# Eight of the sixteen weight halves of a graph kernel are loaded and split during the node stage instead of the prologue

## The reference

```python
# layer 1: graph convolution with self loops
H = X @ W
out = segment_sum(H[src] * (dinv[src] * dinv[dst])[:, None], dst) + b
x = layernorm(x + leaky_relu(out, 0.01))
# layer 2: attention of each edge's target to the edge
r = concat([x[src], x[dst], edge_feat]) @ Wr.T + br
q, k, v = x @ Wq.T + bq, r @ Wk.T + bk, r @ Wv.T + bv
a = softmax_over_edges_of_dst((q[dst] * k).sum_per_head / 8)
out = segment_sum(v * a, dst) @ Wo.T + bo
x = layernorm(x + batchnorm(x + out))
```

## Time and profile before

| | us |
|---|---|
| median of 3 runs | 1370.69 |
| lowest and highest run | 1368.41, 1375.07 |
| the profiled execution | 1368.55 |
| its span, first to last instruction | 1366.8 |
| PE busy in the span | 1293.5 (95%) |
| DVE, POOL, ACT busy | 1079.3, 815.7, 631.2 |

### The profile page before, as it was taken

One profiled execution on the slowest core, in us unless ns is written; L12 is line 12 of the kernel. 1 busy time (PEld: TensorE's weight loads), 2 busy tenths in 40 slices (PEclk: granted clock), 3 DMA queues, 4 the chain that ended last, 5 costly groups with the idle time before them and its releaser, 6 DMA issues. The chain is left out here.

```text
span 1366.8 us, 21920 instructions
## 1 busy us (share of the span) xinstructions
PE 1293.5 (95%) x6534; PEld 1044.9 (76%) x6534; DVE 1079.3 (79%) x2018; ACT 631.2 (46%) x1187; POOL 815.7 (60%) x752
## 2 busy tenths in 40 slices
PE   7898989999999799999999999999999999869987
PEld 6787878888888688888888888888888888644333
DVE  6577638999998425788988888888888888968877
ACT  3477646777777412223332333222332233246877
POOL 3566426667676534556655666666666654567875
PEclk9999999999999799999999999999999999969999
DMA  8798875777776423434344444444444443839886
GB/s 265 261 342 304 269 238 186 241 246 239 247 243 226 168 79 85 133 98 146 117 132 128 133 129 138 139 133 131 137 139 139 139 139 93 289 120 371 276 282 229
DMA packets 128301, 257.96 MB, mean 189 GB/s; under 512 B 21459, under 2 KB 21907, under 8 KB 128114
## 3 DMA queue, kind: packets, MB, share of 16 engines
q1 hardware_dynamic: 97490, 175.31, 38.9%
q0 software_dynamic: 29920, 80.38, 20.2%
q10 hardware_dynamic: 832, 1.57, 0.4%
HBM read 197.18 MB, written 73.60 MB: 198 GB/s over the span
## 5 line engine op out<-in xcount | busy, mean ns | idle before, releaser
L207 PE MATMUL ps<-w_lo,w_hi 128*128 128x512 f32 (+2 forms) x1140 | 415.3, 364 | 6.4 <-DVE w_lo L1457 3.6
L208 PE MATMUL ps<-w_hi,w_lo 128*128 128x512 f32 (+2 forms) x1140 | 410.0, 360 | 0.0
L209 PE MATMUL ps<-w_hi 128*128 128x512 f32 (+2 forms) x1140 | 409.8, 359 | 0.0
L207 PEld LDWEIGHTS ps<-w_lo,w_hi 128*128 128x128 f32 x1140 | 216.7, 190 | 38.7 <-DVE w_lo L1457 4.9
L209 PEld LDWEIGHTS ps<-w_hi 128*128 128x128 f32 x1140 | 216.4, 190 | 32.1
L208 PEld LDWEIGHTS ps<-w_hi,w_lo 128*128 128x128 f32 x1140 | 217.0, 190 | 29.9
L1241 POOL TENSOR_TENSOR acc_x<-acc_x,node_rows 128x512 f32<-128x512 f32 x72 | 116.0, 1610 | 81.2 <-DMA node_rows<-x_table 77.0
L907 POOL TENSOR_TENSOR node_y<-node_z,node_x 128x512 f32<-128x512 f32 x79 | 102.8, 1301 | 72.1 <-issue 38.9
L207 PE MATMUL ps<-w_lo,agg_hi 128*128 128x512 f32 x316 | 132.0, 418 | 1.5 <-DVE agg_lo L971 1.5
L209 PE MATMUL ps<-w_hi,agg_hi 128*128 128x512 f32 x316 | 125.1, 396 | 0.0
L208 PE MATMUL ps<-w_hi,agg_lo 128*128 128x512 f32 x316 | 124.5, 394 | 0.0
(11 more groups left out here) (271 smaller groups left out, 2887.5 us busy)
## 6 DMA issues: line engine op xcount, KB each, us to landing
node_x<-in_x SPq DMA_DIRECT2D x79, 256.0 KB, 3.8
x_table<-node_x SPq DMA_DIRECT2D x79, 256.0 KB, 2.1
node_rows<-x_table SPq DMA_DIRECT2D x79, 256.0 KB, 8.3
coef_all<-coef_table SPq DMA_DIRECT2D x38, 512.0 KB, 7.1
edge_part<-part SPq DMA_DIRECT2D x40, 256.0 KB, 4.2
out_dram<-rows_over_w_lo SPq DMA_DIRECT2D x40, 256.0 KB, 6.2
node_x<-in_ea SPq DMA_DIRECT2D x38, 256.0 KB, 4.9
msg_table<-dst_rows_and_msg SPq DMA_DIRECT2D x38, 256.0 KB, 4.9
```

The costliest lines, as they stand in the source:

```text
L207: pe.matmul(to, left[0], right[1], start=first, stop=False, skip_group_check=onto)
L208: pe.matmul(to, left[1], right[0], start=False, stop=False, skip_group_check=onto)
L209: return pe.matmul(to, left[0], right[0], start=False, stop=last, skip_group_check=onto)
```

## The change

Halves 0 to 7 are handled as before (`EARLY = 8`). Halves 8 to 15 leave the prologue on SP, ACT and DVE. In the node stage SP loads them whole, one every eight steps (half 8 ahead of step 11, the others at steps 16, 24, ... 64). From step 16 to step 79 each step splits one piece of 128 columns: ACT copies it to `w_hi` between `agg_hi` and the root, and POOL subtracts it one step later, behind its gather. PE waits for the 64 pieces in front of the edge stage's first product. Semaphores are renumbered to match.

```diff
+EARLY = 8
+PIECE = 128
 # prologue, SP / ACT / DVE
-            if j + 6 < 2 * NW:
+            if j + 6 < EARLY:
                 load_weights(j + 6)
-            if j < LATER:
+            if j + 2 < EARLY:
                 weights_high(j + 2)
-            if j < LATER:
+            if j + 2 < EARLY:
                 weights_low(j + 2)
 # node stage
+        FIRST_PIECE = 16
+        AFTER_PIECES = FIRST_PIECE + (2 * NW - EARLY) * WH // PIECE
+        def has_piece(j):
+            return not isinstance(j, int) or FIRST_PIECE <= j < AFTER_PIECES
 # SP
+            if isinstance(j, int) and j == 11:
+                load_later(0)
+            if s == 0 and not (isinstance(j, int) and (j < FIRST_PIECE or j + 8 >= AFTER_PIECES)):
+                sp.wait_ge(later_in, (j - FIRST_PIECE) * 2 + 16)
+                load_later((j - FIRST_PIECE) // 8 + 1)
 # POOL, behind the gather
+            if has_piece(j - 1):
+                pool.wait_ge(g.w_hi_ok, j - FIRST_PIECE + EARLY)
+                nc.gpsimd.tensor_tensor(piece(g.w_lo, j - 1), piece(g.over_lo, j - 1), piece(g.w_hi, j - 1).bitcast(F32), ALU.subtract).then_inc(g.w_lo_ok, 1)
 # ACT, between agg_hi and the root
+            if has_piece(j):
+                if s == 0:
+                    act.wait_ge(later_in, (j - FIRST_PIECE) * 2 + 16)
+                nc.scalar.copy(piece(g.w_hi, j), piece(g.over_lo, j)).then_inc(g.w_hi_ok, 1)
 # PE, in front of the edge stage's first product
+                pe.wait_ge(g.w_lo_ok, EARLY + (2 * NW - EARLY) * WH // PIECE)
```

More of the change, by code:

```diff
@@ L49 @@
 WH = K * D // 2
-LATER = 2 * (NW - 1)
+EARLY = 8
+PIECE = 128
 HOMES = 12
@@ L314, in prologue_stage @@
         RUNS, ENDS, CARRIED, CARRY_TURNED, COUNTED, TURNED, DEGREES, ROOTS, DINV_DST = 2, 4, 5, 6, 7, 8, 9, 10, 11
-        w_in = g.w_in = [sem(f"weights_in{s}") for s in range(NW)]
-        w_hi_ok, w_lo_ok = sem("weights_high"), sem("weights_low")
+        w_in = g.w_in = [sem(f"weights_in{s}") for s in range(5)]
+        w_hi_ok, w_lo_ok = g.w_hi_ok, g.w_lo_ok = sem("weights_high"), sem("weights_low")
         def by_k(row):
@@ L433, in weights_high @@
             if i < 2:
-                act.wait_ge(w_in[(0, NW - 1)[i]], 16)
+                act.wait_ge(w_in[(0, 4)[i]], 16)
             else:
-                act.wait_ge(w_in[i // 2], 48 if i // 2 == NW - 1 else 32)
+                act.wait_ge(w_in[i // 2], 32)
             nc.scalar.copy(g.w_half(g.w_hi, i), g.w_half(g.over_lo, i)).then_inc(w_hi_ok, 1)
@@ L461, in scalar_program @@
         for i in range(2):
-            g.load_half(act, g.w_half(g.over_lo, i), i).then_inc(w_in[(0, NW - 1)[i]], 16)
+            g.load_half(act, g.w_half(g.over_lo, i), i).then_inc(w_in[(0, 4)[i]], 16)
             act.dma_start(ea_rows[:, i, :], g.ea[i * P:(i + 1) * P, :]).then_inc(ea_in[i], 16)
@@ L864, in node_stage, with piece @@
         ps_t, ps_o = ps[0:2], ps[4:8]
+        later_in = g.later_in = sem("later_weights_in")
+        FIRST_PIECE = 16
+        AFTER_PIECES = FIRST_PIECE + (2 * NW - EARLY) * WH // PIECE
+        def has_piece(j):
+            return not isinstance(j, int) or FIRST_PIECE <= j < AFTER_PIECES
+        def piece(half, j):
+            return half[:].rearrange("p w n -> p (w n)")[:, bass.ds((j - FIRST_PIECE) * PIECE + EARLY * WH, PIECE)]
         b_in = g.const_in
@@ L883, in sync_program, with load_later @@
     def sync_program(sp):
+        def load_later(i):
+            g.load_half(sp, g.w_half(g.over_lo, i + EARLY), i + EARLY).then_inc(later_in, 16)
         def step(j, s, on):
+            if isinstance(j, int) and j == 11:
[3 more added lines that the diff above has]
+                load_later((j - FIRST_PIECE) // 8 + 1)
             if on(0) and not (isinstance(j, int) and j < RX):
@@ L1868, in finish_stage @@
         SCALE_IN_PSUM, SCALE_ROW = 1, 2
-        y_out = g.w_in[2:6] + g.row_out + g.u_out
-        y_before = [32] * 4 + [16 * NB] * 4
+        y_out = g.w_in[1:5] + g.row_out + g.u_out
+        y_before = [32] * 3 + [16] + [16 * NB] * 4
         mine = g.step_v
```

## The result

The changed kernel takes 1363.42 us in the median of nine runs (1357.95 to 1367.62), the kernel before 1370.93 us beside it (1368.19 to 1375.07). The ratio is 0.994, 95% interval 0.9922 to 0.9959: a gain of 0.41 to 0.78%, or 5.6 to 10.7 us. The forecast was 1365.4, a gain of 5.3, which lies just under that interval. The profiled execution of the changed kernel is the slowest of its nine, 1367.62 us (span 1365.9), so the two profiles are compared stage by stage and not by their ends.

A forecast was written before the change was run, and what follows sets the result against it. PE was taken as the bound, with only its idle time to win: six prologue waits for DVE's scans give -5.3 us, the node stage costs 0, so 1370.69 - 5.3 = 1365.4 us, range 1359 to 1372.

The forecast's parts named there:

- The six waits: Prologue, 98 to 151 us: PE waits 5.3 us for DVE's scans, queued behind a subtraction waiting for ACT's rounding; all disappear.
- The wait changes hands: Prologue rival: the gathers or ACT's scaling take over PE's 5.3 us, so no change; half the gain left gives 1368; 13%.
- The term of 5.3 us: Prologue: removing the six PE waits gains 5.3 us, bounds 0 and 5.3 + 1.3, and arrives at the node stage.
- Traffic at nothing: Prologue: eight loads of 0.5 MB leave SP and the queue; no PE wait names a transfer, so counted at nothing.
- cost 0: Node stage: the added ACT copy, POOL subtraction and loads cost nothing; a step stays at 3.24 us.
- POOL's piece: Node stage: a subtraction of 128 columns on POOL, taken as 0.40 us, standing until node_agg ends.
- over 0.8: Node stage: node_agg longer than 0.8 us was named as a sign of a wrong prediction; 0.75 was expected.
- The sum: Node stage, POOL's step: piece runs 0.40 after node_agg ends, node_y begins some 0.5 behind; POOL needs 2.92 of 3.24 us.
- The slower rival: Node stage: POOL's piece holds DVE's node_agg (16 us, 1381) or sets the step (37 us, 1402); 10%.
- the 0.72: Node stage: POOL has room for a piece of 0.40 + 0.32 = 0.72 us; above that it sets the step.
- 0.58 a step: Node stage: a piece taking the full 1.30 makes POOL's step 3.82 us, adding 0.58 in each of 64 steps.
- the order mends itself: Node stage: node_y is tied to node_agg's end, so delaying one moves the other and the piece keeps arriving behind node_agg.

The follow-up runs named there:

- first: The changed kernel with the eight loads left in the prologue, only the splitting in the node stage: 1364.48 us, ratio 0.9968 to the kernel before.
- sixth: Loads in the prologue, twelve halves instead of eight split in the node stage, in 48 pieces of 256 columns: 1366.96 us, ratio 0.9986 to the kernel before.
- fourth experiment: Loads in the prologue, node-stage pieces of 512 columns in 16 steps instead of 128 in 64: 1381.08 us, ratio 1.0098 to the kernel before.
- third: The changed kernel with DVE instead of POOL subtracting each piece, directly behind node_agg: 1363.31 us, ratio 0.9964 to the kernel before.
- seventh: The changed kernel, with the six halves left in the prologue's loop subtracted one step later: 1361.44 us, ratio 0.9948 to the kernel before.
- fifth experiment: The changed kernel with POOL's piece between node_y and the gather instead of behind the gather: 1362.56 us, ratio 0.9953 to the kernel before.

## Why the prediction was right, and where its sizes were off

**The mechanism.** Right in the main. The six waits are gone, nothing took their place, the gain reached the node stage, and moving only the subtraction in DVE's order gives half of it. The prediction gave the waits this one cause; the loads are a second (below). That the time lies in the range says little, for the range of 1359 to 1372 holds no change too; the waits and the experiments carry the account. "The wait changes hands" is refuted: PE has no wait from 98 to 151 us.

**The term of 5.3 us.** Too small, and the step that failed is taking PE's recorded waits as the whole price of standing. Steps 8 to 15 got 6.58 us shorter for 5.35 recorded, 0.2 more at each of six waits. At the earlier trace rows the group of transposes in front began at 102.25,

```profile
102.25 0.60 PE L606 MATMUL ps<-ident,acc_x 128*128 128x128 f32 x4
```

and the next at 104.18, 1.93 later; undisturbed the pitch is 0.43, so the stall cost 1.50 and not 1.33. A last matmul's recorded 0.60 lies 0.17 over the pitch, and hides that much of the idle time behind it. (The Trainium skill, Perfetto Trace Analysis, section "Tensor Engine Instruction (MATMUL, LD_WEIGHTS)", says that the end of a matmul is computed and not observed. The rows agree: the recorded 0.60 outlasts the next start by 0.17.) The waits' price should have been read as pitch against pitch: 5.3 + 6 x 0.2 = 6.5.

**Traffic at nothing.** This was wrong. Steps 8 to 15, in the profiled execution of each kernel:

| loads of halves 8 to 15 | splitting of halves 8 to 15 | steps 8 to 15, us | PE idle in them |
|---|---|---|---|
| prologue | prologue (kernel before) | 52.9 | 5.35 |
| prologue | prologue, subtraction a step later | 49.6 | 2.49 |
| prologue | node stage (first, sixth and fourth experiment) | 47.3, 48.8, 49.5 | 0.70, 1.90, 2.75 |
| node stage | node stage (the change; third, seventh and fifth experiment) | 46.3, 46.3, 46.3, 46.5 | 0 |

With the splitting gone, the loads still cost 1.0 to 3.2 us. No wait of PE names a transfer; it stands one or two links behind PE, under ACT's or the scans' name: from 60 to 150 us ACT stands 4.7 to 11.3 us for the stores of the sums with the loads in the prologue, and 0 to 1.6 without. Whether the stores are late from the traffic or from their place behind the loads on SP, no run tells. The forecast did not suffer, by luck: the change takes the splitting and the loads away together, and the recorded waits held the price of both.

**The earlier start.** The loop began 2.08 us earlier, which no term had. It also began 1.1 to 2.1 us earlier in the seven other kernels, one of which is the kernel before itself up to the loop's start. So 1.4 of it (49.37 against 50.77) appeared without any of the change: the start differs that much from one execution to another.

**The node stage.** Right in what counts: cost 0, step 3.24, `node_agg` 0.75 in most steps. The first `node_agg` was to come at 190 and came at 186.58, by the two items above. ACT's copy took 0.31 us, not 0.25, and was hidden. POOL's piece takes 0.46 to 0.47 alone, not 0.40, and yet `node_y` starts 0.30 behind `node_agg` and not 0.5: some 0.15 of the piece lies beside `node_agg`'s end. The sum had counted all of it behind. In the changed kernel 7 of 79 `node_agg` took 0.85 to 1.05 us (the prediction had named over 0.8 as a sign of being wrong), 1.3 us too long in all, and PE has no recorded wait for them. The rule of the Trainium skill that was weighed there (SBUF — State Buffer, "Who interferes with whom") agrees with both orders seen: the piece 751 ns where it came second, `node_agg` 2.17 where the piece ran first. The page also infers that DVE's `tensor_tensor` takes only the read side of that interface and that generating descriptors needs the write side; carried over to `node_agg`, which has two SBUF inputs as well, a gather should not hold it, and the 0.75 beside a gather agrees.

**The slower rival.** Pieces of the size that it named do lose, but more than it was priced. Pieces of 256 (0.76 us alone, over the 0.72) lost 7.2 us in the profiled execution where the excess over POOL's room gives 48 x 0.04 = 2; POOL's round with a free piece of 256 takes 3.14 of 3.24, so the room was larger than worked out, and the loss is `node_agg` held. Pieces of 512 lost 16.9 us where the prediction's 0.58 a step gives 16 x 0.58 = 9.3. The working had let `node_y` overlap what it waits for: once the piece goes first, `node_agg`'s rest is one more link in the ring. Its statement that the order mends itself held in most steps with pieces of 128, and in none of the first 14 with pieces of 512.

**Open.** With a piece of 256 behind the gather, `node_agg` is long though it starts well ahead of the piece: 24 that started 0.25 to 0.67 us into a gather, while 21 that started 0.18 to 0.25 into one kept their 0.75. With the piece ahead of the gather none is long, at 0.16 to 0.96. So it is the piece queued there, not the gather, but how it comes to delay a `node_agg` before its own recorded start no run tells; POOL's recorded starts may not be the true ones. Why with 512 columns the piece wins against an earlier `node_agg`, and with 128 loses, is open as well.

## What to carry to other kernels

An instruction whose result is needed late should not stand, waiting for another engine, ahead of one that is needed now: look in the busiest engine's waits for the name behind which it waits, and one link back for what that engine stood for. Moving such an instruction one step later gave 0.28% [0.13, 0.42] at no other edit, and moving half of them, with their loads, to a stage with idle engines 0.6% [0.41, 0.78]. A wait's name is not its only cause: take one cause away at a time before calling the others nothing. A filler in a ring of waits is free only while it fits into the engine's idle time and holds nobody else's instruction; where it holds one, that becomes a link of the ring, and the price is more than the filler's excess. So split fillers fine and place them where they meet nothing.

## What was not expected of the hardware

- A recorded PE wait understates its price: 5.35 us of idle time, 6.58 us of loop.
- A subtraction of fp32 with two SBUF inputs on POOL takes 463 ns for 128 columns, 0.76 us for 256 and 1.30 us for 512: some 2.2 ns a column, and 0.18 us fixed (worked out from the three). On DVE 128 columns take 0.23 us from start to start.
- POOL's gather (0.97 us) and DVE's two-input `node_agg` overlap freely (0.75 us in all 68 meetings with the piece ahead of the gather); a subtraction of 256 columns queued behind that gather made `node_agg` up to 0.64 us longer.
